# Thirty-six tiles in place of thirty-nine in a mixture-of-experts block, four of them made of two 64-row halves

## The chip, the cores and the metric

The kernel runs on one core of a Trainium2 chip. The metric is the device time of one execution in microseconds (us), the median of a few runs. The core has five engines that run side by side and wait for each other on semaphores: TensorE (PE, matmuls), VectorE (DVE), ScalarE (ACT), GpSimd (POOL, which here issues the indirect transfers) and SyncE (SP, which issues plain transfers). Each engine works through its own list in order.

## The reference, cut to what matters

The input is 2048 tokens of 256 numbers. A gated cross-attention over a few sets comes first; the second part is a mixture of eight experts, and each token goes to the two with the highest logits:

```python
def _moe_forward(x, gate_w, gate_b, fc1_w, fc1_b, fc2_w, fc2_b, alpha):
    xf = x.reshape(-1, H_)                        # 2048 x 256
    logits = xf @ gate_w + gate_b                 # 8 experts
    top_val, top_idx = jax.lax.top_k(logits, 2)
    gate_score = jax.nn.softmax(top_val, axis=-1)
    comb = einsum('tk,tke->et', gate_score, one_hot(top_idx)) * alpha[:, None]
    # for each expert, weighted by its row of comb, all added up:
    h = gelu(xf @ w1 + b1)                        # 256 -> 1024
    y = h @ w2 + b2                               # 1024 -> 256
x = x + tanh(g_xattn) * cross_attention(layernorm(x), ...)
x = x + tanh(g_ffn) * moe(layernorm(x), ...)
```

## The kernel before

The attention, the routing and a table that sorts the 4096 pairs of token and expert take the first 80 us or so. The rest is a loop over tiles. A tile is up to 128 rows of one expert; the experts come in the order of their row counts, and each one's last tile is filled up with rows that are thrown away. How many rows an expert gets is known only on the chip, so the loop has as many tiles as the worst case needs: (2 x 2048 - 8) // 128 + 8 = 39 (line 49), used or not.

What a tile i passes through, engine by engine:

- GpSimd fetches its 128 rows from DRAM by an indirect transfer (`fetch_rows`, L1578), five tiles ahead; SyncE transposes them (L415) into one of four slots of `xT`.
- TensorE does `fc1` in eight chunks of 128 hidden units (L635). Numbers are split into a high and a low f16 half, so a chunk is six matmuls with 128x128 weights and 128 moving columns (the rows of the tile). `fc2` (L655) has the activations as weights and w2 as the 256 moving columns: three matmuls for each of eight chunks, summed up in one PSUM bank.
- ScalarE applies gelu to the hidden units in two halves of four chunks, one instruction a chunk since each has its own bias (`gelu`, L919), and weighs the tile's result (`weigh`, L927).
- VectorE writes the high and low half of the activations (`split`, L1488 and L1490), picks bias and weight of the tile's expert for the next tile (`fetch`, L1467 and L1469) and adds b2 to the result (`add_bias`, L1479).
- GpSimd adds the tile's rows to the output in DRAM by an indirect transfer that accumulates (`add_tile`, L1586). It waits until the add before has landed, since two tiles can hold the same token.

TensorE's list interleaves them: the turn of tile i holds, chunk by chunk, `fc1` of tile i and, behind chunks 0 to 3, the second half of `fc2` of tile i-2, behind chunks 4 to 7 the first half of `fc2` of tile i-1 (`tile`, L694). VectorE's turn i (L1498 to L1518) is `fetch(i + 1)`, `add_bias(i - 2)`, `split(i, 0)`, `split(i, 1)` and then, in some turns, `weights_lo` (L1352), with which it and ScalarE (`weights_hi`, L842) turn an expert's f32 weights into f16 halves a few tiles before they are used. `split(i, 1)` waits for the second gelu, and that one for chunk 7 of `fc1` of tile i. Weights lie in 17 regions of `wreg`; which region a tile uses is a number read from a table into a register, so TensorE and VectorE address the weights through registers.

Of the kernel before, what the change touches and what calls it, by code (L numbers as in the profile page):

```python
# [13 lines left out]
P = 128  # L14
# [19 lines left out]
def flamingo_block(nc, x, ctx_sets, token_sets, g_xattn, g_ffn, desc, w_q, b_q, gate_w, gate_b,  # L34
# [14 lines left out]
    TILES = (2 * T - E) // P + E  # L49
# [12 lines left out]
    assert KC == 2 and HALVES == 2 and D == 256 and NG == 4 and FC == 8 and TILES == 39  # L62
# [8 lines left out]
    with ExitStack() as stack:  # L71
# [29 lines left out]
        iota_ti = early[:, 9 * D + P:9 * D + P + TILES].bitcast(I32)  # L101
        iota_pi = early[:, 9 * D + P + NS:9 * D + P + NS + 1].bitcast(I32)
# [123 lines left out]

        mb = maskbias[:, :, :].rearrange("p h n -> p (h n)")
        b1cur = mb[:, 0:NX * FC].rearrange("p (s f) -> p s f", s=NX)
        wcur = mb[:, NX * FC:NX * FC + NX]
        xg = xs[:, 0:2 * NXG, :].rearrange("p t d -> p (t d)")[:, 0:NXG * ROW].bitcast(I32).rearrange("p (s w) -> p s w", s=NXG)  # L230
# [96 lines left out]

        x0_ps = sem("x0_ps")
# [19 lines left out]
        for r in range(2, E):  # L348
            units_of_tile[(r - 1) * PER_RANK] = (2 * r,)
            units_of_tile[(r - 1) * PER_RANK + 2] = (2 * r + 1,)  # L350

        def unit_for(i):

            return min(2 * (i // PER_RANK), NU - 2)
# [64 lines left out]
        def _(pe):  # L419
# [192 lines left out]
            def fc1_operands(c, w):  # L612
                return [[whalf[:, bass.ds(w, 1), part * UNIT + k * F + c * P:part * UNIT + k * F + (c + 1) * P].rearrange(
                    "p a f -> p (a f)") for part in range(2)] for k in range(KC)]

            def fc2_operands(c, w):
                return [whalf[:, bass.ds(w, 1), part * UNIT + c * D:part * UNIT + (c + 1) * D].rearrange("p a d -> p (a d)")
                        for part in range(2)]

            def fc1(i, c, ws):  # L620
                half = c // (FC // 2)
# [7 lines left out]
                if c % (FC // 2) == 0 and i >= 2:  # L629
                    pe.wait_ge(gelu_done, 2 * (i - 2) + half + 1)  # L630
                put = bank[2 * (i % 2) + half][:, c % (FC // 2) * P:(c % (FC // 2) + 1) * P]
                for k in range(KC):
                    hi, lo = ws[k]
                    for n, (w, x_part) in enumerate(((hi, 0), (hi, 1), (lo, 0))):
                        mm = pe.matmul(put, w, xT[:, i % NX, x_part, k, :],  # L635
                                       start=(k == 0 and n == 0), stop=(k == KC - 1 and n == 2))
# [3 lines left out]
            def fc2(i, c, ws):  # L640
                yb = bank[ypos[i % 2]][:, 0:D]
# [17 lines left out]
            def regions(i, n):  # L659
                if i == 0:  # L660
# [5 lines left out]
                    return [(at[0], at[1]) for j in range(n)]  # L666
# [5 lines left out]
                return [(at[2 * j], at[2 * j + 1]) for j in range(n)]  # L672

            def final_tile(i, w, w_1, w_2):

                for c in range(FC // 2, FC):
                    ops2 = fc2_operands(c, w_2[1])
                    for op in ops2:
                        pe.lower_ap(op)
                    fc2(i - 2, c, ops2)  # L680
                for c in range(FC):
                    ops1 = fc1_operands(c, w[0])
                    ops2 = fc2_operands(c - FC // 2, w_1[1]) if c >= FC // 2 else None
                    for k in range(KC):
                        for op in ops1[k]:
                            pe.lower_ap(op, for_matmul_weights=True)
                    if ops2:
                        for op in ops2:
                            pe.lower_ap(op)
# [4 lines left out]
            def tile(i, w, w_1, w_2):  # L694
                if i == TILES - 1:
                    return final_tile(i, w, w_1, w_2)
                for c in range(FC):
                    back, w_b, c_b = (2, w_2, c + FC // 2) if c < FC // 2 else (1, w_1, c - FC // 2)
                    ops1 = fc1_operands(c, w[0]) if w is not None else None
                    ops2 = fc2_operands(c_b, w_b[1]) if w_b is not None else None  # L700
                    if ops1:
                        for k in range(KC):
                            for op in ops1[k]:
                                pe.lower_ap(op, for_matmul_weights=True)
                    if ops2:
                        for op in ops2:
                            pe.lower_ap(op)
# [6 lines left out]
            for i in range(TILES + 2):  # L714
                if i % 4 == 0 and i < TILES:
                    ws += regions(i, min(4, TILES - i))
                if i >= TILES:
                    ws.append(None)
# [3 lines left out]
                if i == 1:  # L722
                    pe.wait_ge(cols_ready, 2)
                    pe.matmul(bank[6][:, 0:TILES], tokens_at[:, :], is_col[:, :], start=True, stop=True).then_inc(fetch_ps, 1)

        @block.scalar
        def _(act):
# [183 lines left out]
            def gelu(i, half):  # L911
# [3 lines left out]
                if i >= 2:  # L915
                    act.wait_ge(lo_done, 2 * (i - 2) + half + 1)
                for c in range(FC // 2):
                    f = half * (FC // 2) + c
                    op = act.activation(h32[i % 2][:, f * P:(f + 1) * P],  # L919
# [710 lines left out]
```

## Time and profile before

| | |
|---|---|
| median of 3 runs | 304.94 us (304.01 to 310.22) |
| profiled execution | 305.23 us, of which 303.5 us span from the first to the last instruction |
| granted TensorE clock, mean over the span | 0.917 of full speed |
| busy, share of the span | PE 86%, DVE 70%, ACT 59%, POOL 48% |
| chain of work that ended last | PE 61%, DVE 13%, DMA 5% |
| `fc1` matmuls (L635) | 1872, 219 ns each from start to end |
| `fc2` matmuls (L655) | 936, 273 ns each from start to end |

Matmuls are pipelined: each lasts longer than the distance to the next one. So the distance from start to start is what a matmul costs, and a busy share says little of how close TensorE is to its limit. A granted clock of 1.00 is 2.4 GHz, 0.50 is 1.2 GHz.

### The profile page before, as it was taken

The numbers are of one execution on the slowest core, as the hardware profiler recorded it, in microseconds if no ns is written. First come the engines' busy times: TensorE is split into PE (matmuls) and PEld (weight loads), VectorE is DVE, ScalarE is ACT, GpSimd is POOL, SyncE is SP. The second block draws the span as 40 slices with busy tenths as digits, with TensorE's granted clock in tenths as the row PEclk, the third lists the DMA queues.
The fourth block names the chain that finished last, engine by engine and source line by source line (L and its number), as shares of the span: only waits on it lengthen the run. The fifth ranks groups of instructions, "written<-read, shape, count | busy, mean of one in ns | idle before, by whom it ended". The sixth has DMA issues, their size and how long they took to land.

```text
span 303.5 us, 9536 instructions
## 1 busy us (share of the span) xinstructions
PE 261.4 (86%) x3275; PEld 245.3 (81%) x3275; DVE 212.7 (70%) x703; ACT 178.5 (59%) x494; POOL 147.0 (48%) x122
## 2 busy tenths in 40 slices
PE   2999818734799999999999999999999999999910
PEld 2999818634699989999999999999999999999900
DVE  3898799997898777686677668667876555555500
ACT  2143869696674766857766685776666545555400
POOL 2121128994524456673765464454576454444240
PEclk9995955855899999999999999999999999999985
DMA  6999999996414444458355535453444844552320
GB/s 186 323 375 376 380 373 378 374 329 205 110 40 72 71 72 71 74 83 78 58 104 75 88 55 94 81 83 69 74 67 75 85 79 72 86 81 28 37 30 4
DMA packets 46719, 40.94 MB, mean 135 GB/s; under 512 B 23025, under 2 KB 43250, under 8 KB 46546
## 3 DMA queue, kind: packets, MB, share of 16 engines
q1 hardware_dynamic: 38544, 29.62, 33.1%
q0 software_dynamic: 7488, 10.39, 23.1%
q8 instruction: 29, 0.48, 0.6%
q10 hardware_dynamic: 642, 0.33, 0.4%
q14 instruction: 16, 0.13, 0.1%
HBM read 26.10 MB, written 9.37 MB: 117 GB/s over the span
## 4 chain that ended last, share of the span: by engine, by line
PE 61%; DVE 13%; DMA 5%; issue 3%; ACT 3%; POOL 1%; DVEq 0%; POOLq 0%; ACTq 0%
PE bank L635 31%; PE bank L655 29%; DMA out_dram<-xn,add_at 4%; DVE wreg L1105 1%; DVE rows L1096 1%; ACT wreg L842 1%; DVE xs L1075 1%; DMA xs<-xrows,fetch_at 1%; ACT rows L919 1%; DVE earlier L1149 1%; DVE wreg L1352 1%; DVE gmark L1139 1%; POOL out_dram L1586 1%; DVE rows L1488 0%; ACT xTp L906 0%
## 5 line engine op out<-in xcount | busy, mean ns | idle before, releaser
L635 PE MATMUL bank<-xTp,wreg 128*128 128x128 f16 x1872 | 153.1, 219 | 1.4 <-ACT xTp L906 1.4
L655 PE MATMUL bank<-wreg,rows 128*128 x936 | 150.5, 273 | 0.5 <-DVE rows L1490 0.5
L635 PEld LDWEIGHTS bank<-xTp,wreg 128*128 x1872 | 128.7, 98 | 9.8 <-ACT xTp L906 1.7
L919 ACT ACTIVATE rows<-bank,maskbias 128x128 f32<-128x128 f32 x312 | 88.9, 371 | 39.9 <-PE bank L635 20.0
L1586 POOL DMA_INDIRECT out_dram<-xn,add_at x39 | 65.7, 1685 | 86.5 <-DMA out_dram<-xn,add_at 54.6
L655 PEld LDWEIGHTS bank<-wreg,rows 128*128 128x128 f16 x936 | 79.1, 98 | 4.5 <-issue 0.6
L1488 DVE TENSOR_SCALAR rows<-rows 128x512 f16<-128x512 f32 x78 | 36.0, 461 | 41.7 <-ACT rows L919 41.5
L1578 POOL DMA_INDIRECT xs<-xrows,fetch_at x39 | 48.0, 1232 | 23.0 <-issue 11.3
L1490 DVE SCALAR_TENSOR_TENSOR rows<-rows 128x512 f16<-128x512 f32 x78 | 54.0, 692 | 2.7
L927 ACT ACTIVATE xn<-xn,maskbias 128x256 f32<-128x256 f32 x39 | 20.0, 512 | 36.6 <-DVE xn L1479 36.5
L1352 DVE SCALAR_TENSOR_TENSOR wreg<-wreg x14 | 32.1, 2291 | 12.1 <-ACT wreg L842 10.4
L842 ACT ACTIVATE wreg<-wreg x14 | 26.9, 1921 | 2.2 <-DVE wreg L1352 2.0
L1544 POOL TENSOR_TENSOR rs<-ve,neg_half 128x4 f32<-128x4 f32 x8 | 8.4, 1050 | 34.3 <-DVE ve L957 20.4
L1479 DVE SCALAR_TENSOR_TENSOR xn<-bank,xs 128x256 f32<-128x256 f32 x39 | 16.3, 418 | 7.0 <-PE bank L655 6.9
L427 PE MATMUL bank<-ident,xs 128*128 128x128 f32 x32 | 7.2, 383 | 5.9 <-DMA xs<-in_x_dram 5.9
L1552 POOL TENSOR_SCALAR at_col<-iota,place_f,token 128x128 f16<-128x128 f32 x12 | 12.0, 1008 | 0.0
L738 ACT ACTIVATE xTp<-bank 128x512 f32<-128x512 f32 x8 | 4.8, 597 | 12.2 <-PE bank L427 12.1
L440 PE MATMUL bank<-rhs_c,xTp 128*128 128x73 f32 x64 | 11.3, 334 | 0.0
L427 PEld LDWEIGHTS bank<-ident,xs 128*128 128x128 f32 x32 | 6.0, 213 | 5.9 <-issue 5.9
L440 PEld LDWEIGHTS bank<-rhs_c,xTp 128*128 128x128 f32 x64 | 10.6, 251 | 0.1
L1552 POOL TENSOR_SCALAR wreg<-iota,place_f,token 128x128 f16<-128x128 f32 x8 | 8.2, 1035 | 2.7 <-DVE place_f L1197 2.7
L786 ACT ACTIVATE xn<-xs,shift,rs 128x256 f32<-128x256 f32 x16 | 8.3, 588 | 1.5 <-DVE shift L1092 1.5
(208 smaller groups left out, 232.1 us busy)
## 6 DMA issues: line engine op xcount, KB each, us to landing
wreg<-in_L_ffn_fc_w_dram SPq DMA_DIRECT2D x16, 1024.0 KB, 13.0
xrows<-rows SPq DMA_DIRECT2D x4, 528.0 KB, 6.3
xs<-in_x_dram SPq DMA_DIRECT2D x4, 512.0 KB, 9.1
out_dram<-xs SPq DMA_DIRECT2D x4, 512.0 KB, 8.8
xs<-in_L_ffn_fc_b_dram SPq DMA_DIRECT2D x1, 1024.0 KB, 6.1
xs<-xrows,fetch_at POOLq DMA_INDIRECT x39, 3.8
out_dram<-xn,add_at POOLq DMA_INDIRECT x39
xTp<-xs SPq DMA_TRANSPOSE x37, 3.7
```

The lines of the kernel that those rows point to most:

```text
L440: mm = pe.matmul(bank[2 + g % 2][:, q * NR:(q + 1) * NR], xTp[:, j, t, k, :], rhs_c[:, k, :], start=(k == 0), stop=(k == KC - 1))
L635: mm = pe.matmul(put, w, xT[:, i % NX, x_part, k, :], start=(k == 0 and n == 0), stop=(k == KC - 1 and n == 2))
L655: mm = pe.matmul(yb, h, w, start=(c == 0 and n == 0), stop=(c == FC - 1 and n == 2))
L842: act.activation(whalf[:, bass.ds(at[1], 1), 0:UNIT].rearrange("p a n -> p (a n)"), wreg[:, bass.ds(at[0], 1), :].rearrange("p a n -> p (a ...
L919: op = act.activation(h32[i % 2][:, f * P:(f + 1) * P], bank[2 * (i % 2) + half][:, c * P:(c + 1) * P], ACT.Gelu, bias=b1cur[:, i % NX, f: ...
L927: act.activation(y_sb[:, i % 2, :], y_sb[:, i % 2, :], ACT.Copy, scale=wcur[:, i % NX:i % NX + 1]).then_inc(y_ready, 1)
L1352: v.scalar_tensor_tensor(out=whalf[:, bass.ds(at[1], 1), UNIT:2 * UNIT].rearrange("p a n -> p (a n)"), in0=wreg[:, bass.ds(at[0], 1), :].r ...
L1488: v.tensor_scalar(hhi[i % 2][:, c], h32[i % 2][:, c], H_SCALE, None, ALU.mult).then_inc(hi_done, 1)
L1490: v.scalar_tensor_tensor(out=hlo[i % 2][:, c], in0=h32[i % 2][:, c], scalar=H_SCALE, in1=hhi[i % 2][:, c], op0=ALU.mult, op1=ALU.subtract) ...
L1552: op = pool.tensor_scalar(at_col[g][:, j, :], iota[:, :], place_f[:, g, 0, j:j + 1], token[:, n:n + 1], ALU.is_equal, ALU.mult)
L1578: pool.indirect_dma_start(out=xg[:, i % NXG, :], out_offset=None, in_=xrows[:, :], in_offset=bass.IndirectOffsetOnAxis(ap=fetch_at[:, i:i ...
L1586: pool.indirect_dma_start(out=out[:, :], out_offset=bass.IndirectOffsetOnAxis(ap=add_at[:, i:i + 1], axis=0), in_=y_sb[:, i % 2, :], in_of ...
```

## The change

Rows are now counted in halves of 64. An expert with c rows gets its full pairs of halves as ordinary tiles; if it has an odd half left, that half goes into a mixed tile together with the odd half of another expert. The worst case is 71 halves, so 36 tiles: 32 full ones and four mixed ones, which stand at places 25, 28, 31 and 34 of the order whether they hold rows or not.

In a mixed tile every step is done once for each half. `fc1` takes twelve matmuls of 64 columns a chunk. `fc2` takes six matmuls a chunk, each with 64 columns of activations as weights, writing partitions 0 to 63 or 64 to 127 of the result. gelu takes two instructions a chunk, `add_bias` two, and the add into the output two transfers in a row, the second waiting for the first. The first half's weights are read in place, the second half's are copied by VectorE into a fixed buffer ahead of time: `keep_w1` (four copies of 128x1024 f16) at the end of the turn before the mixed tile, `keep_w2` (four more) at the end of its own turn. TensorE waits for them (`w1_kept`, `w2_kept`). VectorE builds a table of the halves in 14 small steps in turns 5 to 18 (`odd_halves`), TensorE looks their tokens up with six small matmuls behind tile 17, and the conversions of the weights are moved to earlier turns, some of them in consecutive ones. The diff, cut to its core:

```diff
-    TILES = (2 * T - E) // P + E
+    H = P // 2
+    HALF_TILES = (2 * T + E * (H - 1)) // H
+    TILES = (HALF_TILES + 1) // 2
+    MIXED_AT, MIXED_STEP, MIXED = 25, 3, E // 2
...
-        for r in range(2, E):
-            units_of_tile[(r - 1) * PER_RANK] = (2 * r,)
-            units_of_tile[(r - 1) * PER_RANK + 2] = (2 * r + 1,)
+        first_of_rank = (0, 4, 8, 12, 16, 19, 22, 25)
+        for k, i in zip(range(4, NU), (4, 6, 8, 10, 12, 14, 16, 17, 19, 20, 22, 23)):
+            units_of_tile[i] = (k,)
...
             def fc1(i, c, ws):
...
+                if c == 0 and i in mixed_of:
+                    pe.wait_ge(w1_kept, mixed_of[i] + 1)
+                rows_each = P // len(ws)
+                for h, of_half in enumerate(ws):
+                    at = c % (FC // 2) * P + h * rows_each
+                    put = bank[2 * (i % 2) + part_f][:, at:at + rows_each]
+                    for k in range(KC):
+                        hi, lo = of_half[k]
+                        for n, (w, x_part) in enumerate(((hi, 0), (hi, 1), (lo, 0))):
+                            mm = pe.matmul(put, w, xT[:, i % NX, x_part, k, h * rows_each:(h + 1) * rows_each],
+                                           start=(k == 0 and n == 0), stop=(k == KC - 1 and n == 2))
...
             def fc2(i, c, ws):
...
+                if c == 0 and i in mixed_of:
+                    pe.wait_ge(w2_kept, mixed_of[i] + 1)
...
-                for n, (h, w) in enumerate(((hp, ws[0]), (hp, ws[1]), (lp, ws[0]))):
-                    mm = pe.matmul(yb, h, w, start=(c == 0 and n == 0), stop=(c == FC - 1 and n == 2))
+                rows_each = P // len(ws)
+                for n, (h_part, w_part) in enumerate(((hp, 0), (hp, 1), (lp, 0))):
+                    for h, of_half in enumerate(ws):
+                        at = slice(h * rows_each, (h + 1) * rows_each)
+                        mm = pe.matmul(yb[at, :], h_part[:, at], of_half[w_part],
+                                       start=(c == 0 and n == 0), stop=(c == FC - 1 and n == 2))
...
+                    for h, bias in enumerate(biases):
+                        at = slice(h * rows_each, (h + 1) * rows_each)
+                        op = act.activation(h32[i % 2][:, f * P:(f + 1) * P][:, at],
+                                            bank[2 * (i % 2) + half][:, c * P:(c + 1) * P][:, at], ACT.Gelu,
+                                            bias=bias[:, f:f + 1], scale=1.0 / (X_SCALE * W_SCALE))
...
+            def keep_w1(m):
+                if m == 0:
+                    v.wait_ge(w_lo, NU - 2)
+                    v.wait_ge(out_init, 16 * NG)
+                if m >= 1:
+                    v.wait_ge(fc1_ps, 2 * (MIXED_AT + MIXED_STEP * (m - 1)) + 2)
+                at = nc.values_load_multi_w_load_instructions(
+                    tw_m[0:1, 2 * m + 1, :], engines=[mybir.EngineType.DVE], min_val=0, max_val=NU,
...
+                for part in range(2):
+                    for k in range(KC):
+                        c = slice(part * UNIT + k * F, part * UNIT + (k + 1) * F)
+                        op = v.tensor_copy(kept_w1[part][k], whalf[:, bass.ds(at[0], 1), c].rearrange("p a n -> p (a n)"))
+                op.then_inc(w1_kept, 1)
+                kept_region[0] = at[1]
+
+            def keep_w2(m):
+                if m >= 1:
+                    v.wait_ge(y_ps, MIXED_AT + MIXED_STEP * (m - 1) + 1)
...
+                op.then_inc(w2_kept, 1)
...
+                if 5 <= i < 18:
+                    odd_halves(i - 5)
+                if i == 18:
+                    odd_halves(13)
+                if i + 1 in mixed_of:
+                    keep_w1(mixed_of[i + 1])
+                if i in mixed_of:
+                    keep_w2(mixed_of[i])
                 for k in units_of_tile.get(i, ()):
...
             def add_tile(i):
                 pool.wait_ge(y_ready, i + 1)
                 if i >= 1:
-                    pool.wait_ge(added, 16 * i)
+                    pool.wait_ge(added, added_by(i - 1))
+                if i in mixed_of:
...
+                    m = mixed_of[i]
+                    pool.indirect_dma_start(
+                        out=out[:, :], out_offset=bass.IndirectOffsetOnAxis(ap=add_m[:, 0, m:m + 1], axis=0),
+                        in_=y_sb[0:H, i % 2, :], in_offset=None, compute_op=ALU.add).then_inc(added, 16)
+                    pool.wait_ge(added, added_by(i) - 16)
+                    pool.indirect_dma_start(
+                        out=out[:, :], out_offset=bass.IndirectOffsetOnAxis(ap=add_m[:, 1, m:m + 1], axis=0),
+                        in_=y_sb[H:P, i % 2, :], in_offset=None, compute_op=ALU.add).then_inc(added, 16)
+                    return
```

## Rows read from the trace of the kernel before

**Rows 1.** A stretch: us, then busy (instructions) of PE, PEld, DVE, ACT, POOL; PEclk, DMA.
```profile
240.00:280.00 40.00, 40.00 (x543) 37.76 (x542) 22.03 (x52) 20.68 (x69) 19.42 (x15) 1.00 0.46 72
```

**Rows 2.** Timeline, one tile and its boundary: start us, us, engine, line, operands.
```profile
258.60 0.50 PE L635 MATMUL bank<-xTp,wreg 128*128 128x128 f16 x6
...
260.72 0.29 DVE L1467 COPY maskbias<-b1T 128x8 f32 x1
260.80 0.22 DVE L1469 COPY maskbias<-xs 128x1 f32 x1
...
263.57 0.49 PE L655 MATMUL bank<-wreg,rows 128*128 x3
263.77 1.14 ACT L919 ACTIVATE rows<-bank,maskbias 128x128 f32<-128x128 f32 x4 [0.99 <-PE bank L635]
263.90 0.50 PE L635 MATMUL bank<-xTp,wreg 128*128 128x128 f16 x6
...
264.95 0.43 DVE L1488 TENSOR_SCALAR rows<-rows 128x512 f16<-128x512 f32 x1 [1.15 <-ACT rows L919]
...
265.42 0.69 DVE L1490 SCALAR_TENSOR_TENSOR rows<-rows 128x512 f16<-128x512 f32 x1
...
266.40 0.17 DVE L1467 COPY maskbias<-b1T 128x8 f32 x1 [0.30 <-issue]
```

**Rows 3.** The page's costliest groups, ScalarE: busy us, mean ns of one.
```profile
L919 ACT ACTIVATE rows<-bank,maskbias 128x128 f32<-128x128 f32 x312 | 88.9, 371 | 39.9 <-PE bank L635 20.0
...
L927 ACT ACTIVATE xn<-xn,maskbias 128x256 f32<-128x256 f32 x39 | 20.0, 512 | 36.6 <-DVE xn L1479 36.5
```

**Rows 4.** TensorE's pauses and granted clock: timeline rows and stretches by microsecond.
```profile
54.00:55.00 1.00, 1.00 (x24) 1.00 (x22) 1.00 (x8) 0.00 (x0) 1.00 (x2) 0.52 1.05 380
...
58.64 0.61 PE L576 MATMUL bank<-wreg 128*128 128x128 f16 x8
...
61.00:62.00 1.00, 0.00 (x0) 0.00 (x0) 1.00 (x8) 1.00 (x3) 1.00 (x2) 0.89 1.09 383
...
284.89 4.42 PE L655 MATMUL bank<-wreg,rows 128*128 x39
...
293.00:294.00 1.00, 0.00 (x0) 0.00 (x0) 0.00 (x0) 0.00 (x0) 0.97 (x1) 0.95 0.00 0
```

**Rows 5.** Warm-up matmuls of L583: one microsecond of them, durations min/median/max.
```profile
56.00:57.00 1.00, 1.00 (x41) 1.00 (x38) 1.00 1.07 355
...
L583 PE MATMUL bank<-ident_h x160: 193/234/242, 50.6 to 57.2; 128*128 128x64 f16 x160
```

**Rows 6.** Matmuls on 64 partitions: timeline, and durations min/median/max in ns.
```profile
30.53 1.26 PE L440 MATMUL bank<-rhs_c,xTp 128*128 128x73 f32 x8
31.73 0.50 PE L477 MATMUL bank<-ctxgw,wT 64*128 64x10 f32 x3
...
32.19 1.11 PE L486 MATMUL bank<-ctx_sb,wT 64*128 64x256 f32 x7
32.94 0.51 PE L477 MATMUL bank<-ctxgw,wT 64*128 64x10 f32 x4
33.38 1.00 PE L440 MATMUL bank<-rhs_c,xTp 128*128 128x73 f32 x7
...
L440 PE MATMUL bank<-rhs_c,xTp x64: 229/275/489, 11.9 to 34.2; 128*128 128x73 f32 x64
...
L477 PE MATMUL bank<-ctxgw,wT x32: 171/254/383, 23.9 to 49.1; 64*128 64x10 f32 x32
...
L486 PE MATMUL bank<-ctx_sb,wT x32: 376/556/792, 24.1 to 48.5; 64*128 64x256 f32 x32
```

**Rows 7.** The last adds on GpSimd (timeline), and a stretch behind the last one.
```profile
288.57 1.55 POOL L1586 DMA_INDIRECT out_dram<-xn,add_at  x1 [3.14 <-ACT xn L927]
...
293.03 1.55 POOL L1586 DMA_INDIRECT out_dram<-xn,add_at  x1 [2.91 <-DMA out_dram<-xn,add_at]
...
295.00:296.00 1.00, 0.00 (x0) 0.00 (x0) 0.00 (x0) 0.00 (x0) 0.00 (x0) 0.50 0.94 113
```

More of the change, by code:

```diff
@@ L48, in flamingo_block @@
     RANKS = CAP // P
-    TILES = (2 * T - E) // P + E
+    H = P // 2
+    HALF_TILES = (2 * T + E * (H - 1)) // H
+    TILES = (HALF_TILES + 1) // 2
+    MIXED_AT, MIXED_STEP, MIXED = 25, 3, E // 2
+    FULL = TILES - MIXED
+    AFTER_MIXED = MIXED_AT + MIXED_STEP * MIXED
+    mixed_of = {MIXED_AT + MIXED_STEP * m: m for m in range(MIXED)}
     W_COMB = D
@@ L326, in flamingo_block @@
         table_ready = sem("table_ready")
+        w1_kept = sem("w1_kept")
+        w2_kept = sem("w2_kept")
+        halves_ready = sem("halves_ready")
+        halves_ps = sem("halves_ps")
+        fetch_m_ready = sem("fetch_m_ready")
+        add_m_ready = sem("add_m_ready")
+        table_m_ready = sem("table_m_ready")
         x0_ps = sem("x0_ps")
@@ L629, in fc1 @@
                 if c % (FC // 2) == 0 and i >= 2:
[L630 to L636, printed above, removed]
+                    pe.wait_ge(gelu_done, 2 * (i - 2) + part_f + 1)
+                if c == 0 and i in mixed_of:
[9 more added lines that the diff above has]
+                                           start=(k == 0 and n == 0), stop=(k == KC - 1 and n == 2))
                 if c % (FC // 2) == FC // 2 - 1:
@@ L665, in regions @@
                         skip_runtime_bounds_check_because="regions NU and 2e + 1 of an expert")[1]
-                    return [(at[0], at[1]) for j in range(n)]
+                    return [[(at[0], at[1])] for j in range(n)]
                 if i == PER_RANK:
@@ L698, in tile @@
                     back, w_b, c_b = (2, w_2, c + FC // 2) if c < FC // 2 else (1, w_1, c - FC // 2)
[L699 to L707, printed above, removed]
+                    ops1 = fc1_operands(c, w) if w is not None else None
+                    ops2 = fc2_operands(c_b, w_b) if w_b is not None else None
                     if ops1:
@@ L724, in _ @@
                     pe.matmul(bank[6][:, 0:TILES], tokens_at[:, :], is_col[:, :], start=True, stop=True).then_inc(fetch_ps, 1)
+                if i == 17:
+                    pe.wait_ge(halves_ready, 2)
+                    pe.matmul(bank[6][:, 64:64 + MIXED], tokens_at[:, :], is_pair[:, :], start=True, stop=True)
+                    for h in range(2):
+                        pe.matmul(bank[6][h * H:(h + 1) * H, 68:68 + MIXED], tokens_at[:, 0:H], is_odd[:, h, :],
+                                  start=True, stop=True)
+                    for h in range(2):
+                        pe.matmul(bank[6][0:H, 72 + h * MIXED:72 + (h + 1) * MIXED], tokens_at[:, h * H:(h + 1) * H], is_pair[:, :],
+                                  start=True, stop=True)
+                    mm = pe.matmul(bank[6][0:H, 80:80 + 2 * MIXED], tokens_at[:, 0:H],
+                                   is_odd[:, :, :].rearrange("p h m -> p (h m)"), start=True, stop=True)
+                    mm.then_inc(halves_ps, 1)
         @block.scalar
@@ L1462, in fetch @@
                         skip_runtime_bounds_check_because="the table holds experts 0 .. E - 1")[1]
-                e = first_expert if i < PER_RANK else experts_ahead[i % 4]
+                of_rows = [(slice(0, P), first_expert if i < PER_RANK else experts_ahead[i % 4])]
+                if i in mixed_of:
+                    m = mixed_of[i]
+                    pair = nc.values_load_multi_w_load_instructions(
+                        te_m[0:1, 2 * m:2 * m + 2], engines=[mybir.EngineType.DVE], min_val=0, max_val=E - 1,
+                        skip_runtime_bounds_check_because="the table holds experts 0 .. E - 1")[1]
+                    of_rows = [(slice(0, H), pair[0]), (slice(H, P), pair[1])]
                 if i >= NX:
```

226 lines of the change are left out of this document (190 added, 36 removed).

## The prediction

> **What bounds the kernel now.** I read the busy time of one stretch of the expert loop first, then the timeline over one tile boundary. In that stretch TensorE is never idle, 40.00 of 40.00 us at a granted clock of 1.00, while VectorE and ScalarE are busy for about half of it [rows 1]. So a tile's price is TensorE's pitch. In the timeline [rows 2] a tile's first chunk of fc1 (six matmuls) starts at 258.60 and the next tile's at 263.90: 5.30 us, eight chunks of 0.66. Everything else hides under it, because fc2 runs late: the halves of tile i are used in tiles i+1 and i+2. The reader should keep one chain of [rows 2] in view: the last fc1 chunk of a tile ends, ScalarE starts its second gelu at 263.77, VectorE splits the result from 264.95 to 266.11 (265.42 + 0.69), while TensorE is already in the next tile since 263.90. That overlap is what the change touches. Behind the loop stand the adds into the output, each waiting for the one before.
>
> **What the change removes.** Three full tiles: 3 x 5.30 = **-15.9 us**. Their adds, fetches and transposes go too, but are hidden under the pitch.
>
> **Pause A, ahead of each mixed tile.** The code asks TensorE to wait for `keep_w1` before the first matmul of tiles 25, 28, 31 and 34. VectorE runs `keep_w1` at the end of its turn for the tile before, behind that tile's second split. The split needs the gelu, and the gelu needs the last fc1 chunk of the same tile. So TensorE must stand still from the end of one tile's fc1 until gelu, split and four copies of 128x1024 f16 are done; everything later on TensorE, the ready fc2 chunks too, is queued behind the wait. In the numbers of [rows 2]: TensorE would go on at 263.90; the split ends at 266.11; with a register load behind it VectorE's next instruction came at 266.40, and `keep_w1` loads registers too. So the pause is 266.40 - 263.90 = 2.5, plus 0.1 for the wake (my allowance, of the order of the gaps in the chain), plus four copies C.
>
> The trace has no f16 to f16 copy. The two small copies start 0.08 apart (260.72, 260.80), so an instruction costs at least about 0.07. The cast of 512 columns f32 to f16 takes 0.43 and an 8-column copy 0.17 [rows 2]: 0.26/504 = 0.52 ns a column, so C = 0.07 + 0.53 = 0.60. At the pace of the two-source subtraction (0.69 for 512) C = 1.14. Below, C could fall to 0.07. I take the cast's slope scaled by the bytes that a column moves (4 in place of 6), 0.35 ns: C = 0.43, four copies **1.7**. Pause A = 2.6 + 1.7 = **4.3 us** (2.9 to 7.2).
>
> The Trainium skill (VectorE: DVE Perf Modes, What auto-detection actually checks) says that a one-source copy in SBUF with both sides 16 bit runs at four elements a cycle. No row here shows such a copy; by it (1024/4 cycles at the page's 0.96 GHz and 0.07 each) four would take an estimated 1.35, each pause would be 0.35 shorter, and the whole sum 2.8 lower.
>
> **Pause B, ahead of the mixed tile's fc2.** It waits for `keep_w2`, which stands behind the mixed tile's own second split. Count from the mixed tile's first matmul. Second gelu starts at 263.77 - 258.60 = 5.17. It is now eight activations of 64 columns instead of four of 128. Four of 128 take 1.14 [rows 2], so eight cost between 1.14 (cost by columns) and 2.3 (by instruction). An activation of 256 columns lasts 0.51 and one of 128 lasts 0.37 [rows 3], so 64 columns save only some 0.07 each: I take 1.6. Then the split, 1.20 (264.91 to 266.11), four copies 1.7 and a wake of 0.1: ready at 9.8. TensorE reaches that fc2 after one pitch, four chunks and one fc1 part: 5.30 + 2.65 + 0.33 = 8.3. Pause B = **1.5 us** (0 to 5).
>
> **The clock.** After pauses like A the trace shows the granted clock falling: the last matmul before a hole ends at 59.25, and in 61 to 62 the clock goes from 1.0 (2.4 GHz) towards 0.5 (1.2 GHz) [rows 4]. At the end it took longer: matmuls end at 289.3, the clock leaves 1.0 within 293 to 294. So a hole of 2.6 can be enough and 4.6 surely is; 4.3 is near the upper one, and I let it fall four times. It comes back late: the dense stream of the warm-up starts at 50.6 [rows 5] and runs at half clock until close to 55, where the stretch from 54 shows 0.52 on average [rows 4], some 4.4 us. Half of that work is lost: **2.2 us** a pause (0 if it holds, 3.4 if pause B adds another fall).
>
> **The halves on TensorE.** fc1 turns six matmuls of 128 columns into twelve of 64. The warm-up stream has that shape: 41 matmuls touch one microsecond while each lasts 0.2, so about 34 start, 29 ns each [rows 5]; twelve take 0.35 against 0.33 for six. Nothing. fc2 turns three matmuls of 256 columns into six, each pair writing partitions 0 to 63 and 64 to 127. Nothing in the trace splits the outputs like this. The nearest rows split the inputs [rows 6]: matmuls on 64 partitions stretch from 0.171 for 10 columns to 0.376 for 256, 0.83 ns a column or 0.213 for 256, yet seven start between 32.19 and 32.94, one per 0.107. So two run side by side, and I take the pairs at the price of one. If the output halves don't, 24 more matmuls of 0.109 (three between 263.57 and 263.90) make 2.6 per mixed tile. Going into those split matmuls costs: the group from 30.53 lasts 1.26 and its last one 0.275, so the last starts at 31.52 and the first split one 0.21 later, against 0.11 inside; on the way out the last starts near 33.20 and the next at 33.38, 0.18 [rows 6]. 0.10 + 0.07 for each of eight chunks: **1.3 us** a mixed tile (0 to 2.6).
>
> **The adds.** A mixed tile adds its halves one after the other. Back to back, adds start 293.03 - 288.57 = 4.46 apart, 1.55 of it issue, the rest waiting for the landing [rows 7]; the data move in about one microsecond (0.94 busy in 295 to 296), so half an add saves at least nothing, at most half of issue and data, and lies between 3.2 and 4.46. Three tiles have four adds, 4 x 4.46 = 17.8; with the pauses three tiles last 15.9 + 9.3 = 25.2, so they hide. Without pauses and falls (15.9 + 1.3 = 17.2) they would be the bound. The last mixed tile, 34, is next to last: one more add in the tail, 1.9 to 4.5, I take **3.5**.
>
> **Hidden.** The halves' table is some 40 small VectorE instructions at tiles 5 to 18 and the unit conversions move closer together; a second split ends at 266.11 and is read from about 269.5 (two tiles after 258.60 and half a chunk), so 3.4 us of lag cost nothing; without that cover each would cost its own length. The doubled bias copies and additions go there too. Six small matmuls behind tile 17 with changes of split: 0.6.
>
> **Sum.** Per mixed tile 4.3 + 1.5 + 2.2 + 1.3 = 9.3, four times 37.2. The profiled run took 305.2 (span 303.5; the median is 304.9, so the profile stands for it). 305.2 - 15.9 + 37.2 + 3.5 + 0.6 = **330.6 us**, 8% slower.
>
> **Rivals.**
> *The clock holds.* Pause A is shorter than the 4.6 after the last matmul; the 2.6 before 61.8 speaks against. 330.6 - 8.8 = 321.8.
> *The output halves take turns* on the array: 330.6 + 10.4 = 341. For it only that no row shows output halves.
> *Copies at the two-source pace*: C = 1.14, 2.8 more for four, in both pauses: 330.6 + 4 x 5.6 = 353. Against: one source, two bytes.
> *Not slower: the copies are all but free* (C = 0.07). Then A is 2.9, B vanishes and the hole is too short for the clock: 4 x (2.9 + 1.3) = 16.8, and 305.2 - 15.9 + 16.8 + 4.1 = 310.2, within 2%. It decides where a mixed tile costs less than (15.9 - 4.1 + 6.1)/4 = 4.5 us over a full one; 2.5 of this is gelu and split, which no speed of the copies removes. Faster by 2% would need 1.4, less than that chain alone, so pause A would have to be absent altogether.
>
> **Chances.** Forecast 0.56, clock holds 0.17, halves in turn 0.10, slow copies 0.08, free copies 0.07, no pause 0.02. A measurement of this kernel can tell about 2% from no change, 6.1 us: slower 0.91, same 0.07, faster 0.02. The range leaves out the slow copies and the last two, and reaches from the clock that holds with quicker copies and switches (321.8 - 4) to the halves in turn: 318 to 342. Around the forecast itself, all signs being the same, it is 324 to 338.
>
> **What would show it.** TensorE idle 4 us ahead of fc1 of tiles 25, 28, 31, 34, ended by VectorE's `keep_w1` copies, 0.43 each; a second hole some 8 us of work later, ended by `keep_w2`; the clock at 0.5 behind the first; the 256-column pairs starting 0.11 per pair; four adds in the tail at intervals under 4.5; full tiles still 5.30. Idle of under 3 us ahead of fc1 would prove the forecast wrong, as would copies near 0.1, a clock of 1.0 throughout, or a pair at 0.22.

## The result and the profile after

The changed kernel takes 331.95 us (median of 4 runs, 331.19 to 332.55) beside 305.75 for the kernel before in the same runs: a ratio of 1.088, 95% interval 1.081 to 1.094; one slow run of the kernel before, 310.22, is left out of the ratio. So it is slower, inside the range of 318 to 342 and 1.4 us from the forecast of 330.6. The profiled execution has a span of 329.4 us (before: 303.5) and a mean granted clock of 0.896 (before: 0.917).

The costliest groups of the page (line, engine, operation, count, busy us, mean ns of one; then the idle time before them and what ended most of it):

```profile
L704 PE MATMUL bank<-xTp,wreg 128*128 128x128 f16 (+1 forms) x1728 | 138.9, 219 | 19.6 <-DVE pick_buf L1682 17.3
L730 PE MATMUL bank<-wreg,rows 128*128 (+1 forms) x864 | 143.2, 279 | 6.1 <-issue 3.1
```

`fc1` is L704 now (L635 before) and `fc2` L730 (L655). TensorE, which waited for nothing in the stretch of [rows 1], stands idle 17.3 us ahead of `fc1`, and what ends it is a line of VectorE, the `keep_w1` copies at L1682. The pauses stand in the timeline. Two of the four, the second first (start us, us, engine, line, operands, idle before and its releaser):

```profile
240.16 1.14 ACT L1008 ACTIVATE rows<-bank,maskbias 128x128 f32<-128x128 f32 x4 [0.90 <-PE bank L704]
241.34 0.43 DVE L1701 TENSOR_SCALAR rows<-rows 128x512 f16<-128x512 f32 x1 [1.43 <-ACT rows L1008]
241.80 0.69 DVE L1703 SCALAR_TENSOR_TENSOR rows<-rows 128x512 f16<-128x512 f32 x1
242.51 0.43 DVE L1682 COPY xs<-wreg 128x1024 f16 x1
242.85 0.42 DVE L1682 COPY at_col<-wreg 128x1024 f16 x1
...
243.52 0.42 DVE L1682 COPY pick_buf<-wreg 128x1024 f16 x1
244.09 0.48 PE L704 MATMUL bank<-xTp,wreg 128*128 128x64 f16 x6 [3.63 <-DVE pick_buf L1682]
```

This is the chain of [rows 2] with the copies hung behind it: gelu, split, four copies, and only then TensorE. Its last matmul had started at 240.18, so 3.91 us pass from start to start where the kernel before has 0.11; ahead of tiles 31 and 34 it is 3.90 and 3.88. Ahead of tile 25 it is 6.69 (212.46 to 219.15):

```profile
211.42 2.29 DVE L1522 SCALAR_TENSOR_TENSOR wreg<-wreg  x1 [0.68 <-ACT wreg L925]
212.24 0.49 PE L730 MATMUL bank<-wreg,rows 128*128 x3
214.45 0.41 DVE L1701 TENSOR_SCALAR rows<-rows 128x512 f16<-128x512 f32 x1
214.98 1.12 ACT L1008 ACTIVATE rows<-bank,maskbias 128x128 f32<-128x128 f32 x4
216.14 0.65 DVE L1701 TENSOR_SCALAR rows<-rows 128x512 f16<-128x512 f32 x1 [0.54 <-ACT rows L1008]
216.82 0.69 DVE L1703 SCALAR_TENSOR_TENSOR rows<-rows 128x512 f16<-128x512 f32 x1
217.57 0.43 DVE L1682 COPY xs<-wreg 128x1024 f16 x1
219.15 0.48 PE L704 MATMUL bank<-xTp,wreg 128*128 128x64 f16 x6 [6.42 <-DVE pick_buf L1682]
```

When TensorE was done with tile 24, VectorE was still converting the last unit of weights (2.29 us at L1522), and tile 24's first split came behind that. In the stretches behind the four pauses the granted clock (the third figure from the end of a line: 1.00 is 2.4 GHz, 0.50 is 1.2) is far below the 1.00 of [rows 1], with TensorE busy nearly all the time:

```profile
219.00:227.00 8.00, 7.85 (x128) 7.14 (x129) 1.69 (x6) 2.77 (x13) 0.85 (x1) 0.73 0.19 37
244.00:251.00 7.00, 6.91 (x121) 6.33 (x122) 1.57 (x5) 2.33 (x10) 2.00 (x3) 0.77 0.27 50
268.00:276.00 8.00, 7.49 (x129) 6.66 (x130) 1.91 (x6) 3.21 (x15) 3.50 (x3) 0.81 0.25 45
292.00:302.00 10.00, 9.48 (x133) 8.46 (x134) 2.09 (x7) 3.59 (x17) 2.96 (x2) 0.68 0.07 8
```

The second pause of a mixed tile and the output halves, in TensorE's timeline at the `fc2` of tile 28:

```profile
253.60 0.50 PE L704 MATMUL bank<-xTp,wreg 128*128 128x128 f16 x6
255.25 0.27 PE L730 MATMUL bank<-wreg,rows 128*64 x1 [1.15 <-issue]
255.25 0.30 PE L730 MATMUL bank<-xn,rows 128*64 128x256 f16 x1
255.36 0.27 PE L730 MATMUL bank<-wreg,rows 128*64 x1
255.39 0.27 PE L730 MATMUL bank<-xn,rows 128*64 128x256 f16 x1
...
255.70 0.51 PE L704 MATMUL bank<-xTp,wreg 128*128 128x128 f16 x6
...
256.59 0.51 PE L704 MATMUL bank<-xTp,wreg 128*128 128x128 f16 x6
```

The two matmuls of a pair start together, the next pair 0.11 later. But `fc1` chunks start 0.89 apart (255.70, 256.59) where an ordinary turn has 5.30/8 = 0.66: 0.23 more for each change into the halves and back. It happens 28 times: in eight chunks of three mixed tiles, and four times for the last one, whose second four chunks have no `fc1` between them. And the last adds, GpSimd:

```profile
311.63 1.42 POOL L1823 DMA_INDIRECT out_dram<-xn,add_m  x1 [4.07 <-ACT xn L1015]
315.11 1.42 POOL L1827 DMA_INDIRECT out_dram<-xn,add_m  x1 [2.06 <-DMA out_dram<-xn,add_m]
318.89 1.56 POOL L1831 DMA_INDIRECT out_dram<-xn,add_at  x1 [2.37 <-DMA out_dram<-xn,add_m]
```

The half adds of tile 34 cost 3.48 and 3.78 from start to start, a full one cost 4.46 [rows 7].

### The profile page after: what moved, and what is told of

Same layout as the page of the kernel before. It is cut to its first block and busy times, and to the rows that moved or that the text cites. A ratio compares the mean times of both kernels' runs of the same rounds, so it can differ in the third digit from the quotient of the medians.

```text
span 329.4 us, 9694 instructions
## 1 busy us (share of the span) xinstructions
PE 259.2 (79%) x3353; PEld 232.4 (71%) x3353; DVE 223.4 (68%) x759; ACT 174.9 (53%) x499; POOL 149.6 (45%) x122
## 5 line engine op out<-in xcount | busy, mean ns | idle before, releaser
L704 PE MATMUL bank<-xTp,wreg 128*128 128x128 f16 (+1 forms) x1728 | 138.9, 219 | 19.6 <-DVE pick_buf L1682 17.3
L730 PE MATMUL bank<-wreg,rows 128*128 (+1 forms) x864 | 143.2, 279 | 6.1 <-issue 3.1
L704 PEld LDWEIGHTS bank<-xTp,wreg 128*128 x1728 | 115.1, 100 | 34.9 <-issue 26.5
L1008 ACT ACTIVATE rows<-bank,maskbias 128x128 f32<-128x128 f32 (+1 forms) x320 | 86.6, 363 | 59.8 <-issue 35.3
L1831 POOL DMA_INDIRECT out_dram<-xn,add_at x32 | 57.1, 1784 | 85.7 <-ACT xn L1015 67.5
L730 PEld LDWEIGHTS bank<-wreg,rows 128*128 128x128 f16 (+1 forms) x864 | 73.4, 101 | 13.6 <-issue 7.4
L1810 POOL DMA_INDIRECT xs<-xrows,fetch_at x32 | 42.5, 1327 | 20.4 <-issue 9.1
L1015 ACT ACTIVATE xn<-xn,maskbias 128x256 f32<-128x256 f32 x36 | 18.5, 515 | 44.7 <-DVE xn L1662 44.7
L1522 DVE SCALAR_TENSOR_TENSOR wreg<-wreg x14 | 32.1, 2292 | 9.7 <-ACT wreg L925 8.8
L1662 DVE SCALAR_TENSOR_TENSOR xn<-bank,xs 128x256 f32<-128x256 f32 (+1 forms) x40 | 16.7, 417 | 23.9 <-PE bank L730 23.7
L730 PE MATMUL bank<-xn,rows 128*64 128x256 f16 x80 | 15.7, 281 | 0.0
L1823 POOL DMA_INDIRECT out_dram<-xn,add_m x4 | 6.4, 1612 | 18.8 <-ACT xn L1015 18.8
L1827 POOL DMA_INDIRECT out_dram<-xn,add_m x4 | 5.9, 1481 | 7.9 <-DMA out_dram<-xn,add_m 7.9
```

The source lines that it names most:

```text
L704: mm = pe.matmul(put, w, xT[:, i % NX, x_part, k, h * rows_each:(h + 1) * rows_each], start=(k == 0 and n == 0), stop=(k == KC - 1 and n = ...
L730: mm = pe.matmul(yb[at, :], h_part[:, at], of_half[w_part], start=(c == 0 and n == 0), stop=(c == FC - 1 and n == 2))
L1008: op = act.activation(h32[i % 2][:, f * P:(f + 1) * P][:, at], bank[2 * (i % 2) + half][:, c * P:(c + 1) * P][:, at], ACT.Gelu, bias=bias[ ...
L1015: act.activation(y_sb[:, i % 2, :], y_sb[:, i % 2, :], ACT.Copy, scale=wcur[:, i % NX:i % NX + 1]).then_inc(y_ready, 1)
L1522: v.scalar_tensor_tensor(out=whalf[:, bass.ds(at[1], 1), UNIT:2 * UNIT].rearrange("p a n -> p (a n)"), in0=wreg[:, bass.ds(at[0], 1), :].r ...
L1662: op = v.scalar_tensor_tensor(out=y_sb[at, i % 2, :], in0=bank[ypos[i % 2]][at, 0:D], scalar=1.0 / (H_SCALE * W_SCALE), in1=b2_all[at, bas ...
```

## The experiments

Theory: most of the loss per mixed tile is a place in the order, not work. TensorE waits because `keep_w1` and `keep_w2` stand behind a split that needs TensorE's own newest result, and the pause brings the clock down. Rivals: the copies or the halves cost it by their amount, wherever they stand; the clock is slow for another reason; the output halves take turns; the adds bind. All kernels here but the one with all parts ran once, beside the kernel before on the same chip (304.9 to 305.1 there; 303.9 to 306.1 over 13 runs in one case). So a difference of some 2 us between two times says little by itself, and the readings rest on the timelines. The loop starts between 77.99 and 79.84 in the kernels with the change, which share what stands ahead of it, so parts are compared from the first `fc1` to the end of the span as well. All rows are profiled executions:

```
                               time   loop starts   from there to the end
before                        305.23     79.91        223.6
changed                       331.19     78.46        250.9
keep_w1 early                 312.27     78.09        232.4
both early                    310.61     79.84        229.0
pauses filled                 322.72     77.99        243.0
conversions elsewhere         329.32     78.74        248.9
both early, chunks by two     308.42     78.80        227.9
both early, half out          310.17     78.69        229.7
both early, 26/28/30/32       306.35     78.81        225.8
all together                  304.45     78.08        224.4
all together, one add         296.88     79.81        215.3
```

**keep_w1 earlier in its turn.**

The call moves from the end of VectorE's turn i to its beginning, ahead of the splits.

```diff
+                if i + 1 in mixed_of:
+                    keep_w1(mixed_of[i + 1])
...
-                if i + 1 in mixed_of:
-                    keep_w1(mixed_of[i + 1])
```

> The call of keep_w1 is moved from the end of the turn before the mixed tile to its beginning, ahead of the second split. If pause A comes from the queue place behind gelu and split, the four holes ahead of fc1 of tiles 25, 28, 31, 34 (6.7, 3.9, 3.9, 3.9 us in the trace of after, 18.2 us beyond the ordinary distance) go, and with them the stretches at half clock (some 8 us lost in tiles 25, 28, 31, 34); pause B stays: about 305 to 306 us. Rival: the clock falls for other reasons (pause B, the split matmuls), so only the holes go: 313 to 314 us. Rival: the copies only push the split back and the hole moves to the fc2 that waits for it: over 320 us.

Measured: 312.27 us. The same copies, moved from the end of the turn to its beginning, give back 18.9 (18.5 in the loop). Three of the four pauses and of the four falls are gone; the granted clock is 1.00 from 220 to 294, and two of the stretches behind the places of the later pauses show it:

```profile
240.00:250.00 10.00, 8.80 (x140) 7.20 (x136) 5.17 (x13) 5.63 (x22) 6.18 (x5) 1.00 0.37 65
...
284.00:294.00 10.00, 7.22 (x90) 5.62 (x90) 3.96 (x9) 3.70 (x11) 3.76 (x3) 1.00 0.23 27
```

But I had expected 305 to 306, and the total lies near the 313 to 314 of the rival in which the clock falls for other reasons. The clock rows speak against that rival. What is missing is the first pause: it stayed, 3.8 us with its fall, since VectorE converts the last unit in the turn ahead, and the copies stand behind it at the beginning of the next turn too:

```profile
210.62 2.29 DVE L1522 SCALAR_TENSOR_TENSOR wreg<-wreg  x1 [0.90 <-ACT wreg L925]
213.62 0.43 DVE L1682 COPY xs<-wreg 128x1024 f16 x1 [0.71 <-DVE wreg L1522]
```

**keep_w2 early too.**

It stands behind `keep_w1` at the beginning of turn i now.

```diff
+                if i in mixed_of:
+                    keep_w2(mixed_of[i])
...
-                if i in mixed_of:
-                    keep_w2(mixed_of[i])
```

> As the run before, and keep_w2 stands at the beginning of the mixed tile's own turn. If pause B (1.1 to 1.5 us four times) also comes from the queue place alone: 5.3 us less than with keep_w1 moved alone, about 300 us, and no hole over 0.5 us in tiles 25 to 35. Rival: without any pause the adds (about 4.5 us each, a pair of halves 7.3) set the pace of the last eleven tiles and give 2 to 4 us back: 302 to 304.

Measured: 310.61. Each `keep_w2` pause is gone: the turns behind a mixed tile fall from 7.05 to 7.53 down to 6.20 (5.30 and four changes of split at 0.23). Four times 1.3 would be 5.2; in the loop 3.4 arrived. The time is above both expected ones (about 300, and 302 to 304): they were counted without the first pause, which still lasts 4.00 from start to start. The adds of the last tiles now stand nearly back to back (281.32, 286.11, 291.06, 294.37, 298.43), a sign of the next bound.

**The pauses filled.** Nothing moved; ahead of each mixed tile TensorE runs matmuls that nothing reads, so that it waits shorter.

```diff
+                    for n in range(112 if i == MIXED_AT else 66):
+                        pe.matmul(bank[5][:, 0:P], ident_h[:, :], ident_h[:, :], start=True, stop=True)
```

> Everything stays, but TensorE runs matmuls into an unused bank (112 ahead of tile 25, 66 ahead of the others, 128 columns each) while it would stand still in pause A; nothing else of the computation changes. If the granted clock falls because TensorE stands still, it now stays at 1.0 and the tiles behind the pauses need no more than the others: some 8 us less, about 324 us, with the pauses' length unchanged. Rival: the longer tiles 25, 28, 31, 34 come from their doubled matmuls and not from the clock: 332 us, no change.

Measured: 322.72. Every copy, split and wait is where it was: the turns that end in the four pauses took 12.17, 10.36, 9.95 and 9.91 (in the changed kernel 11.88, 10.02, 10.01 and 9.99), and the clock is 1.00 in the same stretches:

```profile
219.00:227.00 8.00, 7.72 (x147) 7.16 (x143) 3.29 (x8) 4.76 (x21) 3.00 (x2) 1.00 0.27 41
244.00:251.00 7.00, 6.05 (x106) 5.58 (x103) 3.96 (x9) 5.04 (x21) 3.03 (x2) 1.00 0.36 61
268.00:276.00 8.00, 7.00 (x110) 5.79 (x107) 5.12 (x13) 4.46 (x18) 3.83 (x3) 1.00 0.34 62
292.00:302.00 10.00, 8.89 (x129) 7.39 (x126) 5.91 (x13) 4.44 (x17) 3.54 (x2) 1.00 0.24 28
```

So the clock's part is shown by itself: 7.9 us in the loop, 8.5 between the times. The turns of tiles 25, 28, 31 and 34, which start with the clock at 0.50 in the changed kernel, fall from 7.36, 6.86, 6.97 and 9.47 to 5.43, 5.42, 5.75 and 6.73: 7.3 us of it, 1.2 to 2.7 a pause.

**The conversions at other turns.** The last four turns with a conversion were 19, 20, 22, 23.

```diff
-        for k, i in zip(range(4, NU), (4, 6, 8, 10, 12, 14, 16, 17, 19, 20, 22, 23)):
+        for k, i in zip(range(4, NU), (4, 6, 8, 9, 11, 13, 14, 16, 18, 19, 21, 23)):
```

> Only the turns in which weights are converted change: 4, 6, 8, 9, 11, 13, 14, 16, 18, 19, 21, 23 in place of 4, 6, 8, 10, 12, 14, 16, 17, 19, 20, 22, 23. If the 3.2 us that tiles 15 to 23 lost and the 2.8 us by which the first pause A was longer than the others come from VectorE falling behind in pairs of consecutive conversions, both shrink: 327 to 328 us. Rival: the small instructions of the halves' table are what delays VectorE: within 1 us of 332.

Measured: 329.32, 2.6 under the changed kernel's median and 1.9 under its profiled run: between the two expectations (4 to 5 less, and less than 1). The first pause is 5.51 in place of 6.69, and still 1.6 longer than the others:

```profile
217.48 0.48 PE L704 MATMUL bank<-xTp,wreg 128*128 128x64 f16 x6 [5.24 <-DVE pick_buf L1682]
```

Tile 22 lasts 5.30 in place of 6.38, but tile 21 lasts 6.46 in place of 6.02: turns 18 and 19 now both have a conversion, and TensorE waits in tile 21 for a split (0.86 at 193.58). So moving the conversions moves the waits, which fits a VectorE that falls behind where conversions crowd. It takes back only a part of them, and the last conversion still stands right ahead of tile 25.

**Chunks two at a time.** From here on against the kernel with both copies early. `fc2` of a mixed tile goes into the halves four times instead of eight.

```diff
+                    by_two = ops1 is not None and w_b is not None and len(w_b) == 2
...
+                    if by_two and c % 2 == 1:
+                        for d in (c_b - 1, c_b):
+                            fc2(i - back, d, fc2_operands(d, w_b))
```

> The kernel with both copies early (310.6 us), and the fc2 chunks of a mixed tile issued two at a time, so TensorE goes into the 64-row output halves and back four times instead of eight per mixed tile. Theory, mode changes cost 0.228 us per in-and-out: 4 x 4 x 0.228 = 3.6 us less, 307.0, with four chunk boundaries per mixed tile at the full 0.6625 pace. If the chain of adds already sets the end, the chunks show it but the total moves by less than 1. Rival, the extra 0.228 belongs to the split matmuls themselves and not to the change: each grouped pair of chunks takes 0.456 over two full ones and the total stays at 310 to 311.

Measured: 308.42. The turns of 6.20 become 5.74, which is two changes of 0.23 less, and tiles 27, 30 and 33 shorten by 0.14 to 0.46. With the pairs of two chunks in a row, twelve full matmuls and twelve split ones take 1.56, two chunks of 0.66 and one change:

```profile
230.03 0.84 PE L704 MATMUL bank<-xTp,wreg 128*128 128x128 f16 x12
...
231.59 0.51 PE L704 MATMUL bank<-xTp,wreg 128*128 128x128 f16 x6
```

The cost belongs to the change of split and not to the matmuls. The expected 3.6 counted four mixed tiles; the edit reaches three, since the last one's chunks go through `final_tile`, which it leaves alone. So 12 changes go, 2.7 us. Of these only 1.1 arrive in the loop: from the last tile's first matmul to the end it is 30.34 now and 28.57 with the chunks one by one, which is the adds.

**One half of the output left out.** The matmuls of `fc2` for the second 64 rows of mixed tiles are left out, so these rows are not computed.

```diff
-                    for h, of_half in enumerate(ws):
+                    for h, of_half in enumerate(ws[:1]):
```

> Both copies early (310.6 us), and in the mixed tiles fc2's matmuls for the second 64 rows are left out, so these rows are not computed. Theory, the two output halves run side by side: the mixed chunks stay at 0.89 us and the total within 1 us of 310.6. Rival, they take turns on the array for part of their time: 24 matmuls per mixed tile go, up to 0.11 each, and the total falls by up to 10 us.

Measured: 310.17, within 0.5 of the kernel that runs both (0.7 more in the loop). With one matmul of each pair gone the chunks keep their pace of 0.89 (232.56, 233.44), and behind the last of them 0.68 returns:

```profile
232.11 0.52 PE L730 MATMUL bank<-wreg,rows 128*64 x3
232.56 0.51 PE L704 MATMUL bank<-xTp,wreg 128*128 128x128 f16 x6
...
233.44 0.51 PE L704 MATMUL bank<-xTp,wreg 128*128 128x128 f16 x6
...
234.12 0.50 PE L704 MATMUL bank<-xTp,wreg 128*128 128x128 f16 x6
```

So the second output half costs nothing beside the first, and the rival in which they take turns falls.

**Mixed tiles at 26, 28, 30 and 32.** Clear of the last conversion, and of the end.

```diff
-    MIXED_AT, MIXED_STEP, MIXED = 25, 3, E // 2
+    MIXED_AT, MIXED_STEP, MIXED = 26, 2, E // 2
```

> Both copies early, and the mixed tiles at places 26, 28, 30 and 32 instead of 25, 28, 31 and 34. Theory, the remaining first pause of 4.0 us comes from unit 15's conversion, which stands before the copies in turn 23: with the first mixed tile one place later the pause goes (under 0.5), its clock fall goes with it (1.5 to 2), and the half add leaves the last two tiles (up to 3): 302 to 304. Rival, the chain of adds: three adds per two tiles are 4.46 + 2 x 3.5 = 11.5 against 10.6 + 1.8 = 12.4 of TensorE work, so the adds are near the bound and with any lag give the gain back: 306 to 308.

Measured: 306.35, the rival's 306 to 308. The turn of tile 24 is 5.30. The first pause, now ahead of tile 26, was expected to go (under 0.5); it is 1.12 in place of 4.00:

```profile
218.81 0.34 PE L704 MATMUL bank<-xTp,wreg 128*128 128x64 f16 x6 [0.84 <-DVE pick_buf L1682]
```

The clock stays at 1.00 from 78 to 289. Of some 8 that pause, fall and tail were worth, 3.2 arrive in the loop.

**All of it together**, with the conversions of the run that moved them.

> Both copies early, chunks two at a time, mixed tiles at 26, 28, 30 and 32, and the unit conversions one turn earlier or later as in the run of the units alone. If each part gives what was measured or worked out for it: 310.6 - 4 (first pause) - 1.7 (its clock) - 3 (tail) - 3.6 (changes of split) = 298, ratio to before 0.975. If the adds set the end, which then pass 11.5 us per two tiles against 11.5 of TensorE work: 302 to 304, ratio 0.99.

Measured: 303.83 us, median of 10 runs, beside 305.1, median of 13, a ratio of 0.9953, 95% interval 0.9924 to 0.9982. That is half a per cent under the kernel before, clear of the scatter but small. In the two profiled executions the loop itself is no shorter (224.4 and 223.6); what they differ by lies ahead of it, where the start of the loop scatters by 1.9 anyway, and I have no cause for the half per cent. So three tiles fewer bought nothing in the loop: the time is the second expectation's, in which the adds set the end. The pause ahead of the first mixed tile is gone (tile 25 lasts 5.30), and the last tile's first matmul stands 192.1 behind the loop's start in place of 201.3; but 32.3 us follow it in place of 22.3. Its two last stretches (PE, PEld, DVE, ACT, POOL busy, clock, DMA), and adds from its timeline:

```profile
270.00:285.00 15.00, 8.67 (x99) 7.26 (x97) 5.83 (x12) 4.61 (x15) 6.15 (x4) 0.98 0.19 20
285.00:302.00 17.00, 0.00 (x0) 0.00 (x0) 0.42 (x1) 0.51 (x1) 3.12 (x2) 0.50 0.20 22
```

```profile
255.14 1.59 POOL L1835 DMA_INDIRECT out_dram<-xn,add_at  x1 [1.51 <-DMA out_dram<-xn,add_m]
261.70 1.54 POOL L1827 DMA_INDIRECT out_dram<-xn,add_m  x1 [3.65 <-DMA out_dram<-xn,add_at]
266.44 1.41 POOL L1831 DMA_INDIRECT out_dram<-xn,add_m  x1 [3.20 <-DMA out_dram<-xn,add_m]
270.29 1.57 POOL L1835 DMA_INDIRECT out_dram<-xn,add_at  x1 [2.45 <-DMA out_dram<-xn,add_m]
```

TensorE does nothing in the last 17 us, each of these adds is released by the one before it, and from 234 to the end the chain of work that ended last goes from add to add. Three adds here take 270.29 - 255.14 = 15.2 where TensorE needs 5.74 + 5.89 = 11.6 for two tiles.

**One add per mixed tile.** In this kernel the second add of each mixed tile is left out, so its second 64 rows never reach the output.

```diff
-                    pool.wait_ge(added, added_by(i) - 16)
-                    pool.indirect_dma_start(
-                        out=out[:, :], out_offset=bass.IndirectOffsetOnAxis(ap=add_m[:, 1, m:m + 1], axis=0),
-                        in_=y_sb[H:P, i % 2, :], in_offset=None, compute_op=ALU.add).then_inc(added, 16)
```

> The kernel with all parts (303.8 us), in which the mixed tiles add only their first 64 rows into the output; the second half's rows are computed and never added. Theory, the chain of adds sets its end from tile 26 on: four adds of 3.4 to 4.2 us go, and the end moves to what TensorE allows, its last fc1 start (270.2) plus the 22.25 that stand behind it in the kernel before, a span of 292.4 and a time of 294. Rival, the last TensorE work and not the adds sets the end: the time stays within 2 of 303.8.

Measured: 296.88, span 295.1: 7.0 less for four transfers of 64 rows, and 9.1 in the loop. Behind the last tile's first matmul stand 22.4 us, as before the change (22.3), in place of 32.3; in the whole kernel 24 of the 36 adds wait for ScalarE and 11 for the add before (with all parts, 14 and 25 of 40). Three of the last four:

```profile
270.70 1.67 POOL L1827 DMA_INDIRECT out_dram<-xn,add_m  x1 [3.72 <-ACT xn L1019]
275.63 1.57 POOL L1831 DMA_INDIRECT out_dram<-xn,add_at  x1 [3.25 <-DMA out_dram<-xn,add_m]
280.11 1.56 POOL L1831 DMA_INDIRECT out_dram<-xn,add_at  x1 [2.91 <-ACT xn L1019]
```

The expected span of 292.4 was counted from a loop that starts at 78.08; this one starts 1.73 later, which leaves 1.0.

## Why the prediction was right

The mechanism was the one predicted. That the total came so close is in part luck: terms taken too low by 5.0 us and others taken too high by 3.1 stand in the sum. In us, the measured ones from the timeline of the changed kernel, pauses without the ordinary distance of two matmuls (0.11 and 0.06):

```
term                          predicted   measured
three tiles fewer               -15.9      -15.9   (full tiles still 5.30)
pause A, four                    17.2       17.9   6.58 + 3.80 + 3.79 + 3.77
pause B, four                     6.0        5.1   1.45 + 1.31 + 1.03 + 1.26
clock, four falls                 8.8        7.3   the four turns, pauses filled
changes of split, 32              5.2        6.4   28 of 0.228
fc1 in halves, four               0          0.5   5.42 against 5.30
one more add in the tail          3.5        2.8   3.48 + 3.78 against 4.46
tiles 0 to 23                     0.6        3.2   15, 17, 21 to 23: 5.6 to 6.4
sum                              25.4       27.3
```

The loop got longer by 27.3; each term is good to a few tenths, so that the sum meets it to a tenth is chance. The spans differ by 25.9, since this loop started 1.45 earlier (78.46 against 79.91), within the scatter of the table above; no cause is put to it.

**Pause A** was right in mechanism. Its three later instances are 3.9 and not 4.3 because of the copies: each lasts the 0.43 that I took, but the next starts 0.34 behind it (242.51, 242.85, 243.19, 243.52), four in 1.36 where I took 1.7. The Trainium skill (VectorE: DVE Perf Modes, What auto-detection actually checks) gave an estimated 1.35 by its four elements a cycle, and the trace agrees.

**The step that failed is "Hidden".** I let VectorE's lag cost nothing, since a second split is read 3.4 us after it ends. That cover exists for `fc2` only. A turn with a conversion lasts VectorE 6.42 (conversions start at 205.00 and 211.42) against TensorE's 5.30, so two in consecutive turns put it behind; TensorE then waited for splits in tiles 21 and 22, 0.6 and 1.0 us longer than the ordinary distance:

```profile
192.68 0.49 PE L730 MATMUL bank<-wreg,rows 128*128 x3 [0.42 <-DVE rows L1703]
...
199.10 0.49 PE L730 MATMUL bank<-wreg,rows 128*128 x3 [0.82 <-DVE rows L1703]
```

And pause A, which has no cover at all, took the lag in full: 6.69 in place of 3.9. That is 4.4 us put at nothing. I had named the price of the lag without its cover, and not seen that the new wait removes that cover. The runs that move `keep_w1`, the conversions and the mixed tiles show parts of it: in the kernel with all parts, where no conversion stands near the first mixed tile, its pause is gone. Of the 3.2 in tiles 0 to 23 the six matmuls behind tile 17 are 0.3, where I took 0.6; the other 1.3 stand in turns whose lengths differ between kernels with the same instructions there (tile 15: 5.30 to 5.87), and have no cause put to them.

**Pause B** came out at 1.1 to 1.5 against 1.5: gelu's eight halves took 1.75 where I took 1.6, the copies less. **fc1** in halves costs next to nothing, as taken: a turn with it and no other cause lasts 5.42 (tile 28 with both copies early).

**The clock** fell four times, as taken, with TensorE idle for 3.6 us in three of the holes and 6.4 in the first. Behind them TensorE worked at 0.50 for 4.1, 3.1, 2.7 and 5.9 us, against the 4.4 of [rows 4] and [rows 5], and the falls cost 1.8 each in the mean against 2.2. **The pairs** run at the price of one, as taken from [rows 6], though those rows split inputs. The change in and out costs 0.23 and not 0.17: [rows 6] had the direction and three quarters of the size, and the last tile has four changes fewer than I counted. The Trainium skill (TensorEngine Tiling (Array Packing), Key Properties) says that changing the tiling mode drains TensorE. The pairs of chunks fit that, with 0.23 saved for each change that goes; that the 0.23 is a drain no row shows.

**The adds** in the changed kernel behave as predicted: hidden between (27 of 40 wait for ScalarE), one half more at the end. The remark that they would be the bound without pauses and falls is what the further runs met: with the pauses going, only 40 to 65 per cent of each gain arrived. The kernel before showed more of it than I read. I called the adds hidden, and TensorE did not wait for them, but 26 of its 39 adds were released by the add before:

```profile
L1586 POOL DMA_INDIRECT out_dram<-xn,add_at x39 | 65.7, 1685 | 86.5 <-DMA out_dram<-xn,add_at 54.6
```

From 232.79 to 269.62 eight adds in a row, a fetch between each two, came 5.26 apart in the mean, at TensorE's pace of 5.30. So the chain had next to no room: the change takes three tiles from TensorE, and the chain has 40 adds in place of 39. My 4.46 for a full add is its price at the quiet end; in the kernel with all parts full adds took 4.5 to 6.6 from 241.95 on, with a fetch of the same engine behind some of them. What of it is the engine's queue and what is other traffic wasn't tried.

## What to carry to other kernels

A wait is as dear as what stands ahead of the awaited work on its engine: 32 copies that cost VectorE 11 us made TensorE stand for 23 and lose 7 more to the clock, because they stood behind work that needed TensorE's newest result. Moving them to the beginning of the turn gave some 20 back. Cutting tiles pays only until the next chain binds; count that one first, here one add more per split tile in a chain of transfers in which each waits for the one before. See what releases that chain already: a chain that mostly waits for itself has little room. The four pauses, of 4 to 7 us, cost 1.2 to 2.7 more each through the clock.

## What the hardware showed beyond that

Two 64-column halves that write different output partitions ran side by side at the price of one (0.11 per pair of 256 columns), while every change between that form and the full one cost 0.23 us, more than two such pairs. An indirect accumulating transfer of 64 rows cost 3.5 to 3.8 at the quiet end against 4.46 for 128: most of its price didn't go with its rows. And dense work whose result nobody reads, in a pause, kept the clock at 1.00 and saved some 8 us with every copy, split and wait left in its place.
